# ScalarE fetches the search windows of every fourth group row by row, in place of a gather on GpSimd

## What is computed

```python
h = x @ w_lin + b_lin
dense[n, j] = h[src of the j-th edge of node n]     # at most 32 edges per node, rest masked
xb = mab(dense, dense, enc..., mask)                # attention over a node's 32 slots, feed-forward
xp = relu(xb @ pma_lin_w + pma_lin_b)
p  = mab(seed, xp, pma..., mask)                    # one query per node pools the slots
dd = mab(p, p, dec...)
out = layernorm(x + relu(nan_to_num(dd)))
```

## Time and profile before

| | |
|---|---|
| median of 3 runs | 4050.09 us |
| profiled execution | 4049.53 us, span 4047.7 us |
| PE / DVE / POOL / ACT busy | 3126.2 / 3055.1 / 3000.5 / 1664.2 us |
| granted TensorE clock, mean | 0.916 of full speed |
| node gathers L615 | 3101, 948 ns each |
| window gathers L572 | 24, 945 ns each |
| SP's row DMAs L536 | 8960 |
| HBM traffic | 90 GB/s |

### The profile page before, as it was taken

The page is one execution under the profiler, slowest core; times in us unless marked ns, Lnnn a source line. Parts: engine busy times, 40 slices in busy tenths (PEclk is TensorE's granted clock), DMA queues, the critical chain, the costliest instruction groups (busy, mean ns, idle before and its releaser), DMA issues.

```text
span 4047.7 us, 105796 instructions
## 1 busy us (share of the span) xinstructions
PE 3126.2 (77%) x30784; PEld 2002.5 (49%) x30784; DVE 3055.1 (75%) x7166; ACT 1664.2 (41%) x3002; POOL 3000.5 (74%) x3168
## 2 busy tenths in 40 slices
PE   7777777777777777877777777777777877877777
PEld 4545454544454445545455454455444554544444
DVE  6777777777777777777777777777777777777876
ACT  3444444444434434444444444444444444444443
POOL 6777777777777777777777777777777777777772
PEclk8899999899999999999999999899998998999888
DMA  6333333333333333333333333333333333333331
GB/s 213 89 89 88 90 90 88 89 88 90 90 88 89 90 88 89 88 90 89 88 89 90 88 89 87 90 89 88 89 89 88 90 87 90 90 88 89 87 108 35
DMA packets 182788, 368.53 MB, mean 91 GB/s; under 512 B 64029, under 2 KB 116549, under 8 KB 182165
## 3 DMA queue, kind: packets, MB, share of 16 engines
q0 software_dynamic: 152048, 315.92, 29.4%
q1 hardware_dynamic: 29797, 45.03, 3.6%
q10 hardware_dynamic: 320, 0.10, 0.0%
HBM read 348.01 MB, written 16.32 MB: 90 GB/s over the span
## 4 chain that ended last, share of the span: by engine, by line
POOL 70%; issue 23%; PE 3%; DVE 1%; DMA 1%; POOLq 1%; ACT 0%; SPq 0%; DVEq 0%
POOL gathered L615 69%; DMA gathered<-node_table,idx 1%; PE ps L809 1%; POOL windows L572 1%; PE ps L732 1%; PE ps L782 1%; PE ps L683 0%; PE ps L720 0%; POOLq L128 0%; DVE xb L1257 0%; POOLq L130 0%; PE ps L837 0%; DVE windows L1086 0%; DVE gathered L1104 0%; DVE probs_diag L1330 0%
## 5 line engine op out<-in xcount | busy, mean ns | idle before, releaser
L615 POOL DMA_INDIRECT gathered<-node_table,idx x3101 | 2941.2, 948 | 951.1 <-issue 938.5
L720 PE MATMUL ps<-ident,gathered 128*128 128x128 f32 x3128 | 601.7, 323 | 615.6 <-DMA gathered<-node_table,idx 611.4
L720 PEld LDWEIGHTS ps<-ident,gathered 128*128 128x128 f32 x3128 | 497.2, 204 | 966.3 <-issue 807.8
L892 ACT ACTIVATE qT<-ps,cols 128x512 f32<-128x512 f32 x391 | 268.7, 687 | 1080.9 <-PE ps L720 1073.2
L1257 DVE SCALAR_TENSOR_TENSOR xb<-ps,cols,h 128x512 f32<-128x512 f32 x391 | 292.6, 748 | 519.2 <-PE ps L782 518.4
L846 ACT ACTIVATE h_apart<-ps 64x512 f32<-64x512 f32 x782 | 462.2, 591 | 452.8 <-PE ps L720 434.2
L1330 DVE STREAM_TRANSPOSE probs_diag<-probs 32x512 f32<-32x512 f32 x784 | 548.9, 700 | 18.4
L782 PE MATMUL ps<-h,ff_diag 128*128 128x512 f32 x782 | 501.4, 729 | 40.5 <-DVE h L1213 40.4
L732 PE MATMUL ps<-probs_diag,gathered 128*64 128x128 f32 x6256 | 452.3, 288 | 81.6 <-issue 80.2
L732 PEld LDWEIGHTS ps<-probs_diag,gathered 128*64 128x64 f32 x6256 | 365.1, 168 | 250.0 <-issue 232.0
L809 PE MATMUL ps<-xb,pma_diag 128*128 128x512 f32 x782 | 459.6, 670 | 33.6 <-DVE xb L1257 28.9
(11 more groups left out here) (203 smaller groups left out, 3368.0 us busy)
## 6 DMA issues: line engine op xcount, KB each, us to landing
windows<-win_table SPq DMA_DIRECT2D x8960, 2.8 KB
gathered<-node_table,idx POOLq DMA_INDIRECT x3101
node_table<-gathered SPq DMA_DIRECT2D x24, 384.0 KB, 3.1
out_rows<-rows SPq DMA_DIRECT2D x5, 416.0 KB
win_table<-in_dst SPq DMA_DIRECT2D x1, 1716.0 KB
win_table<-in_src SPq DMA_DIRECT2D x1, 1716.0 KB
rows<-in_x SPq DMA_DIRECT2D x2, 640.0 KB, 5.4
rows<-in_x SPq DMA_DIRECT2D x1, 768.0 KB, 7.4
```

What stands on the lines that cost most here:

```text
L615: pool.indirect_dma_start(out=gathered[:, s.slot(0, RING), t * ROW:(t + 1) * ROW], out_offset=None, in_=table, in_offset=bass.IndirectOffs ...
L720: mm = pe.transpose(ps[:, bank, p * P:(p + 1) * P], gathered[:, s.slot(0, RING), lo:lo + 2 * ROW - 2:3], ident[:, :])
L892: nc.scalar.activation(qT[:, s.slot(0, 4), :], ps[:, B_Q, :], ACT.Identity, bias=c_("q_b", P)).then_inc(q_sb, 1)
```

## The change

- POOL issues the window gather once, for iteration 4. From iteration 8 on, ACT fetches the rows of buffer 0, with register loads and one-row DMAs as SP does. It does so in 13 steps, lags -19 to -7, at three places of each: before `xp_rows` (place 0), before `qT` (place 1), before the copies to `h_apart` (place 2). The 128 rows are dealt to these 39 places, 9 for the first quad and 10 for each other, so a place issues 3 or 4 rows; where a quad begins, its 32 registers are loaded first (places 0, 0, 1 and 2 of lags -19, -16, -13 and -10). Before the first, ACT waits for DVE's row numbers and for `idx_ready` of the iteration that used the buffer last.
- DVE counts the samples for these iterations at lag -21 and not -15 (`act_rows_of`), and turns the row numbers into a fourth slice of `odd_turned`. Its search waits for one semaphore for each quad in place of one for the gather.
- `wlin` and `sample_i`, two small start-up tiles, lie in parts of `h2` and `windows`.

```diff
+AT_ACT_ROWS = -21
+ACT_FIRST = 2 * PERIOD // 4
+ACT_STEPS = range(-19, -6)
...
-        wlin = sb("wlin", [P, D])
+        wlin = h2[:, 0, 0:D]
...
-        odd_turned = sb("odd_turned", [P, 3, DEG], I32)
+        odd_turned = sb("odd_turned", [P, 4, DEG], I32)
...
+        sample_i = windows[0:SAMPLE_ROWS, 2, 0:SAMPLE_TILES]
...
@@ POOL step
-                if s.has_iteration(AT_STRETCH) and s.slot(AT_STRETCH, PERIOD) == 0 and (s.looped or s.at >= 16 + AT_STRETCH):
+                if not s.looped and s.at == 4 * DIRECT + AT_STRETCH:
                     wait_apart(pool, idx_ready, s.iteration(AT_STRETCH) - 1, pool_passed)
...
@@ ACT
+            PLACES = [(r, i) for r in ACT_STEPS for i in range(3)]
+            QUAD_PLACES = [9, 10, 10, 10]
+            JOBS = [(q, DEG * i // n, DEG * (i + 1) // n) for q, n in enumerate(QUAD_PLACES) for i in range(n)]
+            loaded = [None]
+
+            def fetch_rows(s, place):
+
+                for (r, i), (q, lo, hi) in zip(PLACES, JOBS):
+                    if i != place or s.slot(r, PERIOD) or not (
+                            s.looped or 4 * ACT_FIRST <= s.at - r < 4 * ITS):
+                        continue
+                    if q == 0 and lo == 0:
+                        wait_apart(act, act_turned_ready, s.period(r) - 1, act_passed)
+                        wait_apart(act, idx_ready, s.iteration(r) - 3, act_passed)
+                        if not s.looped:
+                            act.wait_ge(table_in, 64)
+                    if lo == 0:
+                        _, loaded[0] = nc.values_load_multi_w_load_instructions(
+                            odd_turned[DEG * q:DEG * q + 1, 3, :], engines=(mybir.EngineType.Activation,), min_val=0,
...
+                    for j in range(lo, hi):
+                        act.dma_start(windows[DEG * q + j:DEG * q + j + 1, 0, 0:2 * WIN].bitcast(U8),
+                                      win_bytes[:, bass.ds(loaded[0][j], WIN_BYTES)]).then_inc(act_in[q], 16)
...
@@ ACT step
+                fetch_rows(s, 0)
                 if s.has(L_BACK):
...
+                fetch_rows(s, 1)
                 if s.has(0):
                     act.wait_ge(q_ps, s.octet(-1))
...
+                fetch_rows(s, 2)
+                if s.has(0):
                     act.wait_ge(h_ps, s.octet(-1))
...
@@ DVE
+            def act_rows_of(s):
+
+                u = s.iteration(AT_ACT_ROWS)
+                n = s.period(AT_ACT_ROWS) - 1
+                count_rows(u, 0, u - 1)
+                V.tensor_scalar(win_idx[:, 0:1], win_row[:, 0:1], -1.0, float(WIN_BYTES), ALU.add, ALU.mult
+                                ).then_inc(act_idx_ok, 1)
+                wait_apart(dve, act_idx_ok, n, dve_passed)
+                V.transpose(odd_turned[:, 3, :], win_idx[:, 0:1].broadcast_to((P, DEG))).then_inc(act_turned_ready, 1)
...
                 else:
-                    dve.wait_ge(win_in[0], s.period(AT_SEARCH) * 16 + 32)
+                    for q in range(QUADS):
+                        dve.wait_ge(act_in[q], s.period(AT_SEARCH) * (16 * DEG) - 16 * DEG)
...
+                if s.has_iteration(AT_ACT_ROWS) and s.slot(AT_ACT_ROWS, PERIOD) == 0 and (
+                        s.looped or s.at >= 4 * ACT_FIRST + AT_ACT_ROWS):
+                    act_rows_of(s)
```

More of the change, by code:

```diff
@@ L196, in gnn_kernel @@
         win_table = nc.dram_tensor("win_table", (SAMPLES, 2 * WIN), I32).ap()
+        win_bytes = win_table.rearrange("r n -> (r n)").unsqueeze(0).bitcast(U8)
         table = nc.dram_tensor("node_table", (N, ROW), F32).ap()
@@ L273, in gnn_kernel @@
         samples = sb("samples", [P, SAMPLES])
-        sample_i = sb("sample_i", [SAMPLE_ROWS, SAMPLE_TILES], I32)
         sample_f = lnv[0:SAMPLE_ROWS, 0, 0:SAMPLE_TILES]
@@ L347, in gnn_kernel @@
         odd_in = [[sem(f"odd_in{b}{q}") for q in range(QUADS)] for b in range(3)]
+        act_in = [sem(f"act_in{q}") for q in range(QUADS)]
+        act_idx_ok = sem("act_idx_ok")
+        act_turned_ready = sem("act_turned_ready")
         odd_idx_ok = sem("odd_idx_ok")
@@ L416, in gnn_kernel @@
         pe_passed, pool_passed, dve_passed = sem("pe_passed"), sem("pool_passed"), sem("dve_passed")
-        sp_passed = sem("sp_passed")
+        sp_passed, act_passed = sem("sp_passed"), sem("act_passed")
         block = ctx.enter_context(nc.Block())
@@ L522, in _ @@
                              ).then_inc(table_in, 16)
-            win_bytes = win_table.rearrange("r n -> (r n)").unsqueeze(0).bitcast(U8)
             def odd_rows(b, count):
@@ L870, in _ @@
             rows_even(AHEAD, len(ITEMS))
+            PLACES = [(r, i) for r in ACT_STEPS for i in range(3)]
[15 more added lines that the diff above has]
+                            odd_turned[DEG * q:DEG * q + 1, 3, :], engines=(mybir.EngineType.Activation,), min_val=0,
+                            max_val=(SAMPLES - 1) * WIN_BYTES,
+                            skip_runtime_bounds_check_because="a count of the samples, less one, in bytes of a row")
+                    for j in range(lo, hi):
+                        act.dma_start(windows[DEG * q + j:DEG * q + j + 1, 0, 0:2 * WIN].bitcast(U8),
+                                      win_bytes[:, bass.ds(loaded[0][j], WIN_BYTES)]).then_inc(act_in[q], 16)
             def step(s):
@@ L1024, in rows_of @@
                 at = s.slot(AT_ROWS, PERIOD) // OCTS_PER_IT
-                count_rows(u, at, u)
+                count_rows(u, at, u + (at == OCTS_PER_IT - 1))
                 if at == 0:
@@ L1057, in landed @@
                         dve.wait_ge(odd_in[at - 1][q], s.period(AT_SEARCH) * (16 * DEG))
-                else:
-                    dve.wait_ge(win_in[0], s.period(AT_SEARCH) * 16 + 32)
+                elif not s.looped and u < ACT_FIRST:
+                    dve.wait_ge(win_in[0], 32 + 16)
+                else:
+                    for q in range(QUADS):
+                        dve.wait_ge(act_in[q], s.period(AT_SEARCH) * (16 * DEG) - 16 * DEG)
                 return at
@@ L1323, in step @@
                     index_of(searched[0], s.slot(AT_SHIFT, PERIOD) // OCTS_PER_IT)
-                if s.has_iteration(AT_ROWS) and (s.looped or s.at >= 4 * DIRECT + AT_ROWS):
+                if s.has_iteration(AT_ROWS) and (s.slot(AT_ROWS, PERIOD) or s.at == 4 * DIRECT + AT_ROWS) and (s.looped or s.at >= 4 * DIRECT + AT_ROWS):
                     rows_of(s)
+                if s.has_iteration(AT_ACT_ROWS) and s.slot(AT_ACT_ROWS, PERIOD) == 0 and (
+                        s.looped or s.at >= 4 * ACT_FIRST + AT_ACT_ROWS):
+                    act_rows_of(s)
             def to_diagonal(s, pr, first, last):
```

## The result

The changed kernel takes **4019.9 us** (median of 4 runs, 4017.85 to 4021.98); the kernel before, on the same chip, 4050.88 (median of 4 runs). The ratio is 0.9926, 95% interval 0.9914 to 0.9938. The prediction said 4021. The profiled execution took 4019.36 us, its span 4017.6, against 4049.53 and 4047.7 before: 30.2 us less, at nearly the same mean clock (0.921 against 0.916).

What follows compares the result with a forecast made beforehand. POOL's count of instructions, issued without a pause, was taken as the loop's time. Removing 28.8 us from 4049.5, with every other term hidden or nothing, gave 4020.7, stated as 4021 us; range 4014 to 4058.

Steps and rivals of the forecast that it cites:

- POOL's 23 gathers, 28.8 us: On POOL, 23 of 24 window gathers removed at 1.251 us each, 28.8 us saved in all.
- ACT's issue: On ACT, 128 row DMAs and 4 register loads added: 51 us a turn.
- What of it reaches PE: ACT's issue not covered by its idle time or activations: 13 us a turn, within PE's 24.7 us wait for gathers.
- the added wait: On ACT at place 0 of the first fetching step, waits before the load expose a further 1.7 us a turn.
- the 7 us added for scatter at the plain places: On ACT, 0.3 us for each of 24 other places 0 and 2, because the gaps scatter: 7 us a turn.
- The longer loop body on ACT: ACT's loop grows by over 256 instructions; with 3.7 us more at its branch, 17 still fits in 24.7.
- rival B: SP's row fetches, held back while ACT issues, become the pace: about 4360 us, or about 4165; chance 0.15.
- c: Time each ACT row holds SP back: taken as 0.02 us, between 0 and 0.17; SP binds from 0.045.
- rival C: ACT's issue reaches PE in full, little or no gain: about 4068 us, or about 4125; chance 0.10.
- rival D: POOL's instruction slows under ACT's traffic, or the freed slots weren't the pace: no change, 4050 us; chance 0.05.
- The register load: On ACT, 32 registers in 2.12 us, 66 ns each, against a skill page's about 200 ns a register.
- DVE, start-up and DMA engines: Moved counting on DVE (0.4 us a turn), moved start-up tiles and a third more row traffic: all taken as nothing.

Runs made afterwards that it cites:

- p1: The kernel before with nine further small gathers per octet on POOL: 8397.2 us.
- p2: The changed kernel with the same nine further small gathers per octet on POOL as p1: 8366.65 us.
- n2: The changed kernel with PE's 32 small score matmuls of an octet replaced by one: 6399.95 us, 0.9968 of the unedited kernel before.
- n1: The kernel before with PE's 32 small score matmuls of an octet replaced by one: 6279.16 us, 0.9779 of the unedited kernel before.
- e5: The changed kernel, unaltered, where the kernel before takes 6350.31 us: 6415.41 us, ratio 1.0103.
- e3: The changed kernel with each quad's 32 ACT rows in one burst at place 1: 6825.57 us, 1.075 of the kernel before (6353.4 us).
- e4: The changed kernel with each ACT row as two half-row DMAs, 256 a turn: 6886.0 us, 1.0835 of the kernel before (6353.4 us).

## Why the prediction was right, step by step

1. **POOL's 23 gathers, 28.8 us**: right. The turn is 160.17 us as forecast (160.2), the slot 1.25, the idle time "issue"; the spans differ by 30.1, and p1 against p2, where nothing else should matter, by 30.6. The 1.3 to 2.2 us over lie within the scatter of the runs (3 to 7 us); in the profiled pair 1.5 of them are the node gathers' own time.
2. **ACT's issue**: its size was right, with 0.213 us for a row DMA (forecast near 0.23) and 2.145 for a load.
3. **What of it reaches PE** was the mis-sized term, on the safe side. The forecast had 13 us a turn exposed to PE and left 12 of its 24.7 us wait; 20.5 are left. Some 2.9 us show in that wait and 3.5 as waits on ACT, 6.4 us in all, half of the 13 and about the 6.1 that the forecast had for the load places and the added wait. The rule "a plain place is hidden, a load place shows" held: of ACT's 15.6 us a turn on issue, some 13 stand at the four load places. What was too large is the 7 us added for scatter at the plain places (which are 23 and not 24), where ACT idles some 2 us a turn on issue. Place 1 of the third quad, put at 0, does idle 2.9 us in some turns, but no wait of PE for ACT follows it. The errors couldn't reach the time as long as the sum stayed under 24.7.
4. **The longer loop body on ACT** was allowed up to 3.7 us a turn. In the turn shown ACT's next instruction comes 3.1 us behind its branch (2129.4 to 2132.5), where it came after 0.3 before, and PE stands in its own branch of 3.6 us just then. No wait of PE for ACT stands there. The one that is new and comes every turn, 38.5 us at L761, belongs to the fourth register load, 64 us behind the branch, for which the forecast had 1.4 us a turn: it is 1.8.
5. **SP** (rival B): c was taken as 0.02 and comes out at 0.004 us (0.46 / 128) a row of ACT. B binds from 0.045, so it was far off. The 0.17 us of the start-up loads, of 16 KB each, did not carry over to one-row DMAs. The exclusive lock of which the Trainium skill ("Perfetto Trace Analysis", DMA Instruction — HWDGE) speaks costs SP no more than 0.5 us a turn in this trace. In the 6350 us condition, with PE relieved, n2 against n1 allows up to 0.044.
6. **ACT reaching PE** (rival C) did not come where POOL paces. In the 6350 us condition, where POOL doesn't, the change is 1.0% slower (e5), 7.5% with bursts (e3), 8.4% with twice the DMAs (e4), and in e3 PE's waits for ACT show it. The forecast, as every one of its rows, holds for the condition in which the kernel before takes 4050 us. That the kernel has another one was in none of its rivals; that the first measurement fell in the same condition as the rows is luck.
7. **POOL losing the slots again** (rival D) is excluded: the mean of L620 is 946 ns, and its idle time on PE's L737 fell from 6.1 to 1.2 us.
8. **The register load**: 2.145 us for 32 is 67 ns a register on ACT as on SP. The figure of about 200 ns (the Trainium skill, "Runtime: NRT & Kernel Launch", Instruction fetch mechanics) does not hold for these loads. That page's table of terms speaks of registers loaded from HBM, and these come from `odd_turned`, a tile in SBUF, so the rule bore on them less than the forecast made it; it went by the trace.
9. **DVE, start-up and DMA engines**, at nothing: right so far as shown. The rows on ACT's queue take 0.7% of the 16 engines, and POOL's mean instruction went from 947 to 946 ns. (The 82% that the forecast gave for a single engine is 81 by its own numbers.)

## What to carry to other kernels

When one engine's count of instructions is the time, take instructions off it and price each at its whole slot, gap included (0.945 + 0.305 us here), not at its busy time; the rest is to show that the engine that takes the work has slack where others wait for it. Small DMAs at places spread over an engine's steps cost nothing while it waits there anyway, and the same DMAs in bursts or in twice the number are what turns them into a loss (e3, e4, both in the condition in which POOL is not the pace). A wait that comes once a turn is not thereby the loop branch's: find the place in the turn, here that of a register load. A gain of 0.7% that rests on one engine being the pace should be measured more than once and in more than one place: where another engine paced, this one was a loss of 1.0%.

## What the runs showed of the hardware that was not expected

- **A kernel of 4050 us takes 6350 to 6420 us in another condition**, steadily (6342.56 to 6365.82 over 19 runs of one group). POOL's usual gap is unchanged, but SP's and ACT's sequencers stand still at times for 0.7 us or a multiple at instructions that otherwise take 29 to 225 ns (a MOVE at most 45 ns in the one condition, 1398 in the other), and PE's small matmuls stand 1.2 us and more apart. What stops them stays open, and so does whether it is the chip: the record has the same chip number, 3, for runs in both conditions.
- **ACT's sequencer issues row DMAs while its own activation runs** (L899 at 2000.40 under L939 from 2000.30), 0.213 us each.
- **ACT's row DMAs hardly hinder SP's**: 0.004 us on SP for each of ACT's DMAs, at 128 a turn beside SP's 384, in the 4050 us condition.
- **An indirect DMA of 128 rows costs POOL 1.25 us whatever its rows hold**: 64 bytes (p2's L631), the table's row, and the window's 2816 bytes.
